# Adding the feature halves on GpSimd before TensorE sums them, in three norms of a two-layer transformer kernel

## What is computed

```python
x = L0_attn_x
xn = _layernorm(x)
x = x + L0_attn(xn) + L0_ffn(xn)          # linear attention, shared and routed experts
xn = _layernorm(x)                        # the second layer's norm
x = x + L1_attn(xn) + L1_ffn(xn)          # 16 heads, 256 tokens a sequence; gated MLP of 2048

def _layernorm(x, axis=-1, eps=1e-05):
    m = jnp.mean(x, axis=axis, keepdims=True)
    v = jnp.var(x, axis=axis, keepdims=True)
    return (x - m) / jnp.sqrt(v + eps)
```

## Time and profile before

| | us |
|---|---|
| median of 3 runs | 711.01 |
| lowest, highest | 710.66, 711.22 |
| span of the profiled execution | 710.7 |
| TensorE busy | 666.6 |
| VectorE busy | 490.3 |
| ScalarE busy | 390.1 |
| GpSimd busy | 358.0 |

### The profile page before, as it was taken

The page is one execution under the profiler, slowest core; times in us unless marked ns, Lnnn a source line. Parts: engine busy times, 40 slices in busy tenths (PEclk is TensorE's granted clock), DMA queues, the critical chain, the costliest instruction groups (busy, mean ns, idle before and its releaser), DMA issues.

```text
span 710.7 us, 12784 instructions
## 1 busy us (share of the span) xinstructions
PE 666.6 (94%) x4426; PEld 530.7 (75%) x4426; DVE 490.3 (69%) x954; ACT 390.1 (55%) x691; POOL 358.0 (50%) x297
## 2 busy tenths in 40 slices
PE   7999999998979899999999999999999999999996
PEld 4777777887968787677777777777777777776774
DVE  6889876677566667763858595584958386558655
ACT  4654433555446554825755572765475385449173
POOL 3334768866646451652736173545446263326463
PEclk9999999999989999999999999999999999999999
DMA  8566746889854855120034030005202000302100
GB/s 310 179 205 220 273 170 213 288 293 282 281 200 148 309 142 191 40 51 2 1 105 104 2 79 13 1 1 151 59 20 72 2 1 31 90 1 65 27 2 30
DMA packets 66802, 82.72 MB, mean 116 GB/s; under 512 B 7090, under 2 KB 50354, under 8 KB 66738
## 3 DMA queue, kind: packets, MB, share of 16 engines
q1 hardware_dynamic: 63156, 73.39, 32.5%
q0 software_dynamic: 3072, 8.39, 3.6%
q10 hardware_dynamic: 512, 0.13, 0.1%
HBM read 40.34 MB, written 28.84 MB: 97 GB/s over the span
## 4 chain that ended last, share of the span: by engine, by line
PE 61%; DVE 10%; ACT 10%; issue 8%; SPq 4%; DMA 4%; POOL 2%; ACTq 1%; POOLq 0%; DVEq 0%
PE acc L656 5%; PE acc L658 4%; PE acc L657 4%; PE ring L656 3%; PE pm L658 3%; PE pm L656 3%; PE pm L657 3%; PE ring L658 3%; PE ring L657 3%; PE ring L1016 3%; PE pv L656 2%; PE ring L1010 2%; PE pv L658 2%; PE pv L657 2%; PE ring L1043 2%
## 5 line engine op out<-in xcount | busy, mean ns | idle before, releaser
L1617 POOL TENSOR_TENSOR hl<-hf,hh 128x512 fp32r<-128x512 f32 (+1 forms) x76 | 101.9, 1342 | 226.4 <-ACT hh L1297 226.3
L1297 ACT ACTIVATE hh<-hf 128x512 fp32r<-128x512 f32 (+1 forms) x76 | 47.6, 630 | 78.6 <-DVE hf L2172 65.1
L656 PE MATMUL acc<-hh,wh 128*128 128x512 f32 (+1 forms) x168 | 72.0, 428 | 3.0 <-POOL hl L1617 3.0
L2236 DVE TENSOR_REDUCE mx<-ring 128x2 f32<-128x512 f32 (+1 forms) x96 | 61.6, 684 | 8.7 <-PE ring L1016 8.7
L658 PE MATMUL acc<-hl,wh 128*128 128x512 f32 (+1 forms) x168 | 66.6, 396 | 0.0
L657 PE MATMUL acc<-hh,wl 128*128 128x512 f32 (+1 forms) x168 | 66.3, 394 | 0.0
L2172 DVE TENSOR_TENSOR hf<-hf,pv 128x512 f32<-128x512 f32 x64 | 43.6, 681 | 32.1 <-PE pv L658 31.8
L1760 POOL TENSOR_TENSOR pl<-act,ph 128x512 f16<-128x512 f32 x32 | 42.6, 1332 | 32.5 <-ACT ph L1512 29.5
L1489 ACT ACTIVATE hf<-pm 128x512 f32<-128x512 f32 x56 | 33.4, 596 | 43.0 <-PE pm L658 37.2
L656 PE MATMUL pv<-xh,wh 128*128 128x512 f32 x128 | 54.0, 422 | 0.0
L658 PE MATMUL pv<-xl,wh 128*128 128x512 f32 x128 | 51.1, 399 | 0.0
(11 more groups left out here) (299 smaller groups left out, 2032.2 us busy)
## 6 DMA issues: line engine op xcount, KB each, us to landing
w4s<-w4hl SPq DMA_DIRECT2D x16, 512.0 KB, 4.2
ws<-qs SPq DMA_DIRECT2D x12, 512.0 KB, 5.3
qT<-qp SPq DMA_DIRECT2D x96, 64.0 KB, 2.4
kT<-kp SPq DMA_DIRECT2D x96, 64.0 KB, 2.5
xs<-yg SPq DMA_DIRECT2D x2, 2944.0 KB, 13.9
ys<-act SPq DMA_DIRECT2D x22, 256.0 KB, 3.9
stage<-w SPq DMA_DIRECT2D x8, 608.0 KB, 5.3
xh<-xs SPq DMA_DIRECT2D x12, 256.0 KB, 3.7
```

The costliest lines, as they stand in the source:

```text
L656: pe.matmul(o, w_hi, x_hi, start=first, stop=False, skip_group_check=True)
L1297: a.activation(h_parts(n)[0][0:rows, :], hf[0:rows, n % 2, :], ACT.Copy).then_inc(s_hh, 1)
L1617: return pool.tensor_tensor(dst, src, hi.bitcast(F32), ALU.subtract)
L2236: v.tensor_reduce(mx[:, i, h0:h0 + nh], ring[j % 2][:, :].rearrange("p (n k) -> p n k", n=nh), AX.X, ALU.max).then_inc(s_mx, 1)
```

## The change

In the three norms inside the loop, GpSimd first adds the two halves of the tokens, `xg(n)[:, 0, :] + xg(n)[:, 1, :]`, into `xsum` (the buffer `yg` under another name), and TensorE's mean is one matmul on `xsum`. Later GpSimd adds the two halves of the squares in place, and TensorE's variance runs over half 0 alone. There are two new semaphores, `s_xsum` and `s_sqsum`. The norm of n = 4 is left as it was.

```diff
+        xsum = yg[:, :, :].rearrange("p a d -> p (a d)")
...
             def ln_mean(n):
                 m = n - G
-                pe.wait_ge(s_cadd, 4 * (m + 1))
                 if n > G:
+                    pe.wait_ge(s_xsum, m)
                     pe.wait_ge(s_act, T0 * G + (m - 1) * T1 + 10)
+                    pe.matmul(ln_bank(n), ones[:, :], xsum, start=True, stop=True).then_inc(s_mean, 1)
+                    return
+                pe.wait_ge(s_cadd, 4)
                 for k in range(KD):
                     mm = pe.matmul(ln_bank(n), ones[:, :], xg(n)[:, k, :], start=k == 0, stop=k == KD - 1)
                 mm.then_inc(s_mean, 1)
 
             def ln_var(n):
-                pe.wait_ge(s_sq, n - G + 1)
+                halves = 1 if n > G else KD
+                if n > G:
+                    pe.wait_ge(s_sqsum, n - G)
+                else:
+                    pe.wait_ge(s_sq, 1)
                 for i in range(4):
-                    for k in range(KD):
+                    for k in range(halves):
                         mm = pe.matmul(ln_bank(n)[:, i:i + 1], sq[:, k, i * P:(i + 1) * P], ones[:, 0:1],
-                                       start=i == 0 and k == 0, stop=k == KD - 1, skip_group_check=True)
+                                       start=i == 0 and k == 0, stop=k == halves - 1, skip_group_check=True)
                 mm.then_inc(s_var, 1)
...
+            def add_halves(n):
+                pool.wait_ge(s_cadd, 4 * (n - G + 1))
+                if n > G + 1:
+                    pool.wait_ge(s_mean, n - G)
+                pool.tensor_tensor(xsum, xg(n)[:, 0, :], xg(n)[:, 1, :], ALU.add).then_inc(s_xsum, 1)
+
+            def add_squares(n):
+                pool.wait_ge(s_sq, n - G + 1)
+                pool.tensor_tensor(sq[:, 0, :], sq[:, 0, :], sq[:, 1, :], ALU.add).then_inc(s_sqsum, 1)
...
                 split_h(n0 + 6, P)
+                if g < G - 1:
+                    add_halves(G + g + 1)
...
                 split_values(b1)
-                for t in range(10, 13):
+                split_h(n0 + 10, P)
+                if g < G - 1:
+                    add_squares(G + g + 1)
+                for t in range(11, 13):
                     split_h(n0 + t, P)
```

More of the change, by code:

```diff
@@ L256, in transformer_blocks @@
         s_wide = sem("inverse_on_all_partitions")
+        s_xsum, s_sqsum = map(sem, ("feature_halves_added", "square_halves_added"))
         s_v, s_k, s_q = map(sem, ("v_product", "k_product", "q_product"))
```

## The result

| | us |
|---|---|
| kernel before, median of 4 runs on the same chip | 710.84 (710.07 to 711.22) |
| changed kernel, median of 4 runs | 704.49 (704.04 to 705.33) |
| ratio, 95% interval | 0.9915 (0.9901 to 0.9929) |
| predicted | 705.9, range 705.0 to 707.8 |

The change saves 6.35 us; the interval of the ratio makes that 5.0 to 7.0 us. The forecast of 5.1 us was right in its mechanism. The span of the profiled execution fell from 710.7 to 703.0 us.

The account below looks back on a forecast made before the run. TensorE was taken as the bound, with both sums on the path; 0.865 + 0.84 = 1.705 us a place, 5.1 us in three, so 711.0 - 5.1 = 705.9 us, range 705.0 to 707.8.

Parts of the forecast that it names:

- The bound: Norms inside groups 1 to 3 of the second layer: both sums on the path in TensorE's queue, 1.73 and 1.68 us.
- Part 1, the mean: Mean in each of three places: one of two float32 128x512 matmuls goes, saving 0.865 us.
- Part 2, the variance: Variance in each place: four of eight one-column matmuls go, saving 1.68 / 2 = 0.84 us.
- A fixed part: Possible switching cost of 0.11 us within each sum that would not halve, making its saving 0.055 us smaller.
- Parts 3 and 4, the additions: GpSimd's additions of token and square halves in each place: 1.29 us each, in idle time, at no cost.
- Side by side with VectorE: VectorE and GpSimd can hold each other; nm<-mx starts 0.06 us after the second addition, the weakest joint.
- The forecast of 0.27 for an addition of 1.77 us: If the second addition takes 1.77 us, nm<-mx ends late and TensorE's transpose waits: 0.27 us a place, 0.8 in all.
- Does it reach the end?: Behind the sums everything later hangs on TensorE and shifts with it; the smallest slack left is 1.2 us.
- ScalarE's slack at gate 12: ScalarE's idle time before reading gate 12, behind the variance: 2.04 us before, 1.2 us left with the change.
- More than the sum: Rival for the whole kernel: shifted groups meet fewer pauses, for instance, giving 704.8 us; chance 0.02.
- The base of the sum: Whole kernel before the change: 711.0 us taken as start, from a 711.01 us median and a 710.7 us profiled span.

Follow-up runs that it names:

- e2: Against the kernel before: only the mean halved, with GpSimd adding the token halves, variance as before; 718.67 us, ratio 0.9957.
- e3: Against the kernel before: only the variance halved, with GpSimd adding the halves of the squares, mean as before; 718.22 us, ratio 0.9944.
- e4: Against the kernel before: GpSimd's six additions and their waits put in, both TensorE sums left whole; 722.17 us, ratio 1.0004.
- e6: Against the changed kernel: GpSimd's additions left out, sums over the first half of the features alone; 715.04 us, ratio 0.9937 to before.
- e7: Against the changed kernel: a further unused GpSimd addition directly ahead of the addition of the squares; 715.80 us, ratio 0.9941 to before.
- the two later comparisons: The changed kernel run again, unaltered, against the kernel before: 716.99 us, ratio 0.9932, and 713.66 us, ratio 0.9916.
- e14: Against the changed kernel: 60 more TensorE instructions, waits always met, over three passes (40 written in each, half became instructions); 716.11 us.
- e10: Against the changed kernel: 30 more TensorE instructions, waits always met, over three passes (20 written in each, half became instructions); 711.60 us.

## Why the prediction fell short, point by point

- **The bound.** Right. Both sums were on the path in all three places, and TensorE's idle time in a place stayed at 1.16 us.
- **Part 1, the mean.** Right: 0.865 us worked out, 0.86 measured (e2: 0.85 to 0.87).
- **Part 2, the variance.** The mechanism was right, the size not. I halved 1.68 us to 0.84; it was 0.90 (e3). The chain has 1.68 us for sixteen records and 0.79 for eight, so eight more cost 0.89 and the first eight less than that. A fixed part is there, with the opposite sign of the one that I had looked for: the sum is shorter than its records times their price, not longer. Three times 0.06 is 0.18 us of the miss. The 0.34 us of the product behind it, which I had offered as the size of a fixed part, did not change.
- **Parts 3 and 4, the additions.** Right: 1.28 and 1.29 us, free (e4, e6). The predicted idle time behind the first was 2.8 us, measured 2.94.
- **Side by side with VectorE.** Right. The clearance was 0.06 us by the forecast and 0.07 in the trace; e7 shows what lies behind it, 0.69 us in a place. The forecast of 0.27 for an addition of 1.77 us was not tried; its rule, that the operation ends 0.03 us behind the addition, is what e7 shows.
- **Does it reach the end?** Right. ScalarE's slack at gate 12 was 1.57 us, where I had 1.2: the high part ahead of that gelu started at 322.04 where it had started at 325.54, and the gelu of tile 10 at 308.90 instead of 311.10, so the high part moved by 3.50 - 2.20 = 1.30 us against that tile, 0.44 more than the 0.86 of the mean. That is the code packet of before again: its two DMA issues ahead of the high part took 1.58 us, those of after 1.15, and the high part starts 0.1 us behind them in both. So the extra slack comes from where the packet fell in before and not from the change. The slack was not needed.
- **"More than the sum", with a chance of 0.02 and "No row speaks for it".** This is the step that failed: the stretches outside the three places were put at nothing. The page has the queue q8 with instruction packets, and the wait of 0.36 us for kT<-kp stood in the trace of before, in a group that the change doesn't edit. I had not asked what moves when 52 instructions leave the program. It gave 0.3 to 0.7 us in group 4 (66.78 to 67.09 down to 66.40 to 66.47) and took 0.2 to 0.9 us in group 3. In the first pair of profiles that is 0.59 won and 0.40 lost, so it widens the range more than it moves the centre. The time measured is nearest to the 704.8 us of this rival. Group 4 does meet one pause less, but that gives 0.59 us where the rival wants 1.1, and it comes from the position of a packet and not from the shift of the group.
- **The base of the sum.** I took 711.0 as the time and the profiled span as 0.3 us less than a usual run. The changed kernel's profiled execution took 704.77 us for its span of 703.0, and in the other kernels the difference was 1.7 to 1.9 us as well. By that the profiled execution of before would have taken 712.5 us, some 1.5 us more than its median. That doesn't enter the sum, since I took the saving off the median, but it would explain why the spans differ by 7.7 us and the medians by 6.35. The median of before in the comparison was 0.17 us lower than the one I started from.

The terms shown by traces make 5.26 + 0.59 - 0.40 = 5.45 us, against the 5.1 of the forecast, and 710.84 - 5.45 = 705.4 us, which is inside the range. So the mis-sized variance and the code packets do not by themselves explain why the median fell below 705.0. The measured 6.35 us (5.0 to 7.0) includes 5.45, and so do the two later comparisons, with 0.0068 x 722.83 = 4.9 us and 0.0084 x 720.27 = 6.1 us, each to within 2 us. Whether the remaining 0.9 us of the first comparison is more than the scatter of the untouched stretches stays open. My range was too narrow on the side of a larger gain: it allowed 0.9 us beyond the forecast, while code packets of 0.2 to 0.9 us of either sign and the measurement's own 1 us asked for more.

## What to carry to other kernels

Where sums over features run on a full TensorE, let an idle engine add the halves first; the saving arrives whole when the sums stand in the chain, and it is worth asking next whether the sums can run in one pass, which here gave another 3.2 us. Price a repeated matmul by the difference between long and short runs of it, not by an average, and look at what VectorE does within 0.1 us of a new GpSimd operation. An edit that changes the number of instructions also moves later code fetches, so look for DMA issues and waited-for transfers near the instruction packets of the trace, and allow some tenths of a microsecond of either sign in stretches that it never touches.

## What the runs showed of the hardware

- A DMA issue of `qT` or `kT` that began within 0.6 us after the start of a code packet (q8, 0.02 MB) took 0.84 to 1.93 us instead of about 0.60, on SyncE and on ScalarE, in all 90 cases. The packet in group 4 of before, which started 0.33 us after the last issue had begun, left the issues alone, and the transfer landed after 3.1 us instead of 2.4. Where such a delay is waited for it costs 0.2 to 0.9 us of a group, elsewhere nothing. Which resource the packet shares with an issue was not told apart.
- Eight more one-column float32 records cost 0.89 to 0.90 us behind eight that cost 0.79 to 0.81.
- A one-pass fp32r matmul of 128x512 takes 0.24 us to the next product, the float32 one 0.86: 3.6 times as much with two records.
- 20 waits that are met at once (e14, counted as instructions in each pass) lengthen the stretch from the gelu of tile 14 to the next group's first from 11.50 us in the changed kernel to 11.94 to 12.00, so by 0.44 to 0.50 us on a full TensorE. Ten of them (e10) change it by 0.06 at most.
